# Batches 2 to 6: ScalarE's double pieces over two rows, the gate's product over two rows

## The reference

```python
xz = einsum('bld,ed->bel', hidden, in_proj_w)          # 1024 x channels, 1024 z channels
x  = silu(conv4(x) + conv_b)                           # causal, 4 taps, per channel
dt_lo, Bmat, Cmat = split(einsum('bdl,kd->blk', x, x_proj_w))   # 32, 16, 16
delta = softplus(dt_lo @ dt_proj_w.T + dt_proj_b)
h = h * exp(delta * A) + delta * B_t * x_t             # for each token, 16 states a channel
y = sum_over_states(h * C_t) + x * D
out = (y * silu(z)) @ out_proj_w.T
x1 = layernorm(hidden + out)
logits = x1 @ gate_w.T                                 # 8 experts
top2, idx = top_k(logits, 2); w = softmax(top2)
y_all = einsum('td,eod->teo', x1, expert_w) + expert_b
result = layernorm(x1 + sum(y_all[idx] * w))
```

## Time and profile before

| | |
|---|---|
| runs | 2264.38, 2264.75, 2259.15 us |
| profiled execution | 2260.66 us, span 2258.9 us |
| mean granted TensorE clock | 0.947 |
| busy share of the span | TensorE 90%, VectorE 88%, GpSimd 82%, ScalarE 73% |
| the five periods of batches 2 to 6 | from 561.2 to 1863.0 us of the span |

### The profile page before, as it was taken

How to read it: one execution, slowest core, us unless ns; L and a number is a source line. 1 busy time by engine, 2 the same in 40 slices (tenths; PEclk the granted TensorE clock), 3 DMA queues, 4 the chain that set the end, 5 groups by cost and what they waited for, 6 DMA issues and landing times. The chain is left out here.

```text
span 2258.9 us, 30428 instructions
## 1 busy us (share of the span) xinstructions
PE 2036.0 (90%) x8624; PEld 1200.9 (53%) x8624; DVE 1982.8 (88%) x2191; ACT 1658.4 (73%) x3074; POOL 1854.5 (82%) x1505
## 2 busy tenths in 40 slices
PE   8897779898999989999899998999899998879898
PEld 3444455455564555545555555645556455655453
DVE  5899989989999999899999999899998998989912
ACT  5767858767598866979588875988678886667534
POOL 2988999788998889889898889989898997696503
PEclk9897879989899999999999999999999999789999
DMA  5432142367754786557863678557855576495775
GB/s 164 160 108 70 40 148 77 95 212 229 246 126 124 231 289 180 137 171 233 280 172 106 209 249 264 118 153 248 293 150 136 176 245 236 146 272 189 246 270 117
DMA packets 222085, 412.79 MB, mean 183 GB/s; under 512 B 29880, under 2 KB 36152, under 8 KB 221920
## 3 DMA queue, kind: packets, MB, share of 16 engines
q1 hardware_dynamic: 180448, 322.36, 42.6%
q0 software_dynamic: 20496, 57.16, 12.4%
q10 hardware_dynamic: 20976, 31.33, 4.3%
HBM read 299.37 MB, written 85.72 MB: 170 GB/s over the span
## 5 line engine op out<-in xcount | busy, mean ns | idle before, releaser
L1784 ACT ACTIVATE dA<-delta,negA 128x512 f32<-128x512 f32 (+1 forms) x1146 | 714.4, 637 | 317.4 <-DVE hst L1976 250.1
L1925 POOL TENSOR_TENSOR hst<-u,Bbc 128x512 f32<-128x512 f32 x666 | 880.7, 1427 | 57.4 <-PE hTp L1334 36.3
L1976 DVE TENSOR_TENSOR_SCAN hst<-dA,hst 128x512 f32<-128x512 f32 x672 | 790.3, 1207 | 44.0 <-ACT dA L1784 36.8
L1334 PEld LDWEIGHTS hTp<-ident,hst 128*128 128x128 f32 x4096 | 496.2, 149 | 318.4 <-issue 172.2
L1334 PE MATMUL hTp<-ident,hst 128*128 128x128 f32 x4096 | 557.9, 288 | 96.5 <-DVE hst L1976 24.4
L1965 DVE SCALAR_TENSOR_TENSOR y<-hTp,Ct,y 128x1024 f32<-128x1024 f32 x463 | 585.1, 1264 | 54.5 <-PE hTp L1334 51.6
L1925 POOL TENSOR_TENSOR first_dbu<-u,Bbc 128x512 f32<-128x512 f32 x222 | 295.1, 1411 | 16.5 <-DVE hits L2057 11.6
L1976 DVE TENSOR_TENSOR_SCAN hst<-dA,first_dbu 128x512 f32<-128x512 f32 x224 | 263.2, 1207 | 17.7 <-issue 9.1
L1318 PE MATMUL bank<-wslot,hidT 128*128 128x512 f32 x512 | 250.3, 621 | 8.1 <-ACT zs L1666 6.2
L1318 PE MATMUL bank<-wslot,tokT 128*128 128x512 f32 x496 | 233.3, 598 | 4.0 <-ACT tokT L1686 3.9
L1318 PE MATMUL bank<-delta,tokT 128*128 128x512 f32 x480 | 224.4, 600 | 0.0
(11 more groups left out here) (187 smaller groups left out, 2886.7 us busy)
## 6 DMA issues: line engine op xcount, KB each, us to landing
wslot<-in_w_expT SPq DMA_DIRECT2D x90, 1024.0 KB
Bbc<-b_scratch SPq DMA_DIRECT2D x113, 256.0 KB
wslot<-in_w_inT SPq DMA_DIRECT2D x26, 1024.0 KB
y<-scaled POOLq DMA_DIRECT2D x49, 512.0 KB
zs<-sorted_tokens ACTq DMA_DIRECT2D x91, 256.0 KB, 6.1
sorted_results<-ysb SPq DMA_DIRECT2D x90, 256.0 KB
res<-in_w_expT SPq DMA_DIRECT2D x18, 1024.0 KB, 5.7
gate_scratch<-zs SPq DMA_DIRECT2D x64, 256.0 KB, 2.8
```

Of the source, the lines that this page charges most:

```text
L1334: mm = nc.tensor.transpose(hTp[q % 2][:, tok(j)], hst[n % 2][:, j, start:start + P], ident[:, :])
L1784: nc.scalar.activation(decay_of(step, halved), delta[w.odd][:, j, cols], ACT.Exp, scale=negA[:, j, n:n + 1]).then_inc(exp_done, 1)
L1925: nc.gpsimd.tensor_tensor(dbu_row(n, j), u[w.odd][:, j, :], Bbc[n % 2][:, :], ALU.mult).then_inc(dbu_done, 1)
L1976: nc.vector.tensor_tensor_scan(hst[n % 2][:, j, :], dA[j % 2][:, :], dbu_row(n, j), 0.0, ALU.mult, ALU.add).then_inc(scan_done, 1)
```

## The change

Three things are changed, all in the table of batches 2 to 6. ScalarE's double pieces are taken apart (`one_by_one`): the first half stays in its row, the second goes to the next row, behind that row's decay; a piece that stood in a row with a scaling moves one row on; later pieces never overtake earlier ones, so they are pushed along. The gate's product is cut in two: token tiles 0 and 1 stay in row 62, 2 and 3 go to row 64 (`gate_in_two_rows`), and the count is issued as two shares of one row, which leaves its instructions as they were. VectorE's gate moves from row 63 to 65 (`moved_on`), and GpSimd's hold, which follows from it, by two rows.

```diff
+SCALED_ROWS = [2 * (q + NH + 1) for q in BY_DMA]
+def one_by_one(pieces, steps):
+    rows, last = [], 0
+    for row, x, _ in pieces:
+        row += row in SCALED_ROWS
+        for k, name in enumerate(SINGLE.get(x[0], (x[0],))):
+            last = min(max(row + k * (last <= row), last), steps - 1)
+            rows.append((last, (name,) + x[1:], 0))
+    return rows
+def gate_in_two_rows(pieces):
+    rows, later = [], []
+    for row, x, share in pieces:
+        if later and row > later[0][0] - 2:
+            rows, later = rows + later, []
+        if x == ("gate",):
+            rows += [(row, x, 0), (row, x, 1)]
+            later = [(row + 2, x, 2), (row + 2, x, 3)]
+        elif x == ("count",):
+            rows += [(row, x, 0), (row, x, 1)]
+        else:
+            rows.append((row, x, share))
+    return rows
+def moved_on(pieces, piece, by):
+    rows, last = [], 0
+    for row, x, share in pieces:
+        last = max(last, row + by * (x == piece))
+        rows.append((last, x, share))
+    return rows
...
-        self.shares = FINE_SHARES if self.fine else SHARES
+        self.single = self.fine or steps == STEPS
+        self.shares = FINE_SHARES if self.single else SHARES
         order, users, turns = plan(pieces, steps, pace, steps > STEPS, self.fine)
+        if self.single and not self.fine:
+            order["pe"] = gate_in_two_rows(order["pe"])
+            order["dve"] = moved_on(order["dve"], ("gate",), 2)
...
+        if self.single and not self.fine:
+            order["act"] = one_by_one(order["act"], steps)
...
                 elif name == "gate":
...
-                    for t in range(NT) if not w.seg.fine else (share,):
+                    for t in range(NT) if not w.seg.single else (share,):
...
-                    if not w.seg.fine:
+                    if not w.seg.single:
                         piece(w, ("sig3", j))
...
```

More of the change, by code:

```diff
@@ L1471, in piece @@
                             mm = nc.tensor.matmul(ps[:, NT * NE:(NT + 1) * NE], ones[:, :], hits[:, t, :], start=(t == 0), stop=(t == NT - 1))
-                    if share == 1 or not w.seg.fine:
+                    if share == 1 or not w.seg.single:
                         for i in range(NT):
```

## The result

The changed kernel takes 2352.19 us, the median of four runs (2337.69 to 2360.73), against 2264.57 us before (2259.15 to 2268.25, four runs): ratio 1.038, 95% interval [1.032, 1.045]. It is slower, as forecast, but 88 us slower and not 60, and the time lies above the range of 2284 to 2345.

A forecast was written before the change was run, and what follows sets the result against it. No engine was the bound everywhere: VectorE set the pace, with waits for short chains through ScalarE or TensorE. Terms of 4.6, 2.2, 3.0, 0.5, 1.7 and 0 made 12.0 us a period, 60 in five: 2324, range 2284 to 2345.

The forecast's parts named there:

- The rule: ScalarE works in order; each row begins with its decay, which waits for the scan two rows earlier, as do pushed pieces.
- The x stage: Rows 77 to 80: x 5 and x 6 evictions come behind decays 79 and 80, delaying VectorE's taps; 4.6 us a period.
- Sig 7 to row 88: Rows 82 to 88: sig 7 behind decay 82 makes GpSimd's product 2.5 us later, delaying row 88; 2.2 us a period.
- The dt stage: Rows 94 to 100: later evictions delay row 98's sum by 0.8 and TensorE at row 100 by 2.2; 3.0 us a period.
- Neither is won back: The delays at rows 98 and 100 stay, as TensorE is packed, 22.7 of 23.0 us up to row 110.
- Row 15: yT 1's eviction moves behind decay 15, so TensorE's turning starts 0.61 later; 0.5 us a period.
- The z stage: z 0's and z 2's copies come behind decays 40 and 48: 1.0; x 0 and x 2, rows 71 to 74: 0.7.
- The gate: VectorE's waits for product and count vanish (-2.7 us a period) or double (+2.7); z 6 wants z 5's bank sooner; taken as 0.
- The clock: TensorE's waits before xproj and moe 2 exceed 3.5 us each; 3.4 us more at the lower clock would cost 1.7 us.
- Rival C: The clock drops after both longer TensorE waits, before xproj and moe 2: 17 us more, 2341; chance 0.08.
- Rival B: Only the x stage counts, the rest absorbed by waits VectorE has anyway: 23 us, 2287; chance 0.13.
- Rival D: Faster: earlier decays return 24 us, half the gate's waits 7, x evictions cost no more than today: 2233; chance 0.06.

The follow-up runs named there:

- x_only: The kernel before with only sig2/sig3 taken apart and row 78's pieces pushed on: ratio 1.020.
- x_back: The changed kernel with row 78's pieces left in row 78 and sig2 and sig3 in one row again: ratio 1.021.
- xsT_late: The kernel before with the evictions of xsT 2 and 3, and dt2 2 behind them, one row later, behind decay 100: ratio 1.008.
- xsT_warm: As xsT_late, with two more 128x512 products of no use on TensorE in its wait before moe 2: ratio 1.006.
- rest: The changed kernel with sig2/sig3, dt/dt1 and dt2/dt3 in one row again and nothing pushed on from rows 78, 94 and 110: ratio 1.010.
- rest_copy: As rest, but with the copy of z 5 back in row 63 beside its first half: ratio 1.004.
- dt_back: The changed kernel with dt and dt1, dt2 and dt3 in one row again and nothing pushed on from rows 94 and 110: ratio 1.030.
- pieces_only: Of the change only ScalarE's pieces taken apart, with the gate as in the kernel before: ratio 1.039.
- later_three: The kernel before with three whole pieces (ln2 0, ln1 2, dt2 1) one row later: ratio 0.997.

## Why the prediction was wrong

The forecast of slower, the rule about the decays and the largest term were right; the size was a third too small. The step that failed is the one on the clock: it put at nothing the lower clock behind TensorE's longer waits.

- **The rule** (each row begins with a decay, so what is pushed on waits for a scan) held in each place shown.
- **The x stage**, forecast 4.6, measured 4.5 (x_only 4.5, undone by x_back).
- **Sig 7 to row 88**, forecast 2.2, measured 3.5, and 3.1 in x_only. The delay was right: GpSimd's product for sig 7 ends 2.6 us later after row 80's scan, forecast 2.5. Row 88's decay waits behind xproj, and xproj took 1.1 us longer on average, at the lower clock; in batch 4 the wait before it had grown from 1.28 to 3.59. That this is the clock's doing is read from the traces; no run kept the clock up here. Batch 4 also was not like the others here, as the prediction took it to be: before the change the clock fell behind the wait of 1.3 us in batches 2 and 4 and stayed whole behind it in 5 and 6.
- **The dt stage**, forecast 3.0, measured 5.9. Its parts: row 98, forecast 0.8, measured 0.8; TensorE's resumption, forecast 2.2, measured 2.3; then 1.6 for the clock at row 100. That the clock falls by the wait and costs about this much is shown by xsT_late and xsT_warm (0.9 to 1.7), and batch 2 of x_back, where it stayed up behind the same wait, is 1.4 to 1.8 shorter than the other four. Then 0.7, net, for GpSimd's wait for dt 4 at row 110, which I never looked for, and 0.4 in small steps from row 100 on. "Neither is won back" was right, but I had read TensorE's packing from row 100 to 110 as the only limit there. Only the trace shows the part at row 110; no run took it away by itself.
- **Row 15**, forecast 0.5, measured 1.3 for rows 0 to 16, of which 0.6 stand between the scans of rows 14 and 16. In rest, rest_copy, x_back, dt_back and pieces_only, all with yT 1 behind decay 15, that step grew by 0.5 to 0.7 too, and by -0.1 to 0.0 in those without. So the term was right; the rest lies ahead of row 14, in waits that differ from period to period, and has no cause shown.
- **The z stage**, forecast 1.0 up to row 60, measured 0.5: z 0's and z 2's copies do delay TensorE, and the decays of rows 46 and 53, which come earlier, take it back by row 53 (1.0 at row 50, 0.0 at row 53, counted from row 38).
- **The gate**, forecast 0, with x 0 and x 2 at 0.7; measured 1.9 together. By the estimate under rest the gate costs 0.8 and the pieces 1.7 in these rows, and the clock, which was low in them for 20.5 us of five periods instead of 27.3, gave 0.7 back in this execution. The prediction named one cause, z 6 wanting z 5's bank, and priced it at nothing; moved back, the copy of z 5 takes 0.4 of the 2.0 that rest has by the same estimate.
- **The clock** is the step that failed. I forecast that TensorE's waits before xproj and moe 2 would be "over 3.5 us each", had before me in the earlier trace rows a wait of 2.44 with the clock at 0.51 behind it, and still took the higher clock for the likely case, because a wait of 1.24 kept it. The kernel before had more to see: behind the wait of 1.28 before xproj the clock fell in two of the four periods that have this wait. Measured: behind moe 2's wait 1.6 us a period, and behind xproj's about 1.1, together some 13 of the 28 us that were missing; shown by experiment is the part at row 100. Rival C, with both waits followed by the lower clock and 17 us for it, got 0.08; its mechanism was the case, and its 2341 was 11 us too low. The rest of the miss is rows 100 to 127 (1.2 a period), the gate's rows (1.2), rows 0 to 14 (0.7) and small parts, less the 0.5 that the z stage cost too little.
- TensorE's 29.1 us of added busy time look like the 27.8 us that were missing, but that is luck. 5.3 of them lie in rows 76 to 80, whose step was 4.5 in every period, with the clock low for 3.4 to 3.6 us in three and never in two; and row 110's part is not the clock's.
- Rival B (absorption) was wrong: the steps come and go whole. Rival D was wrong too: the waits of rows 15, 46 and 53 did go, 12 us in five periods, but rows 47, 63 and 88 now wait 16 us more, and the x evictions cost what the forecast said. What it was right in is shown by later_three.

On the clock the Trainium skill was weighed in the prediction (TensorE: Matmul & The Clock Gate, "HAM oscillation"). By its rule, waits bring the lower clock back in the midst of a kernel. The traces agree: behind the wait of 3.54 us the clock was at or near 0.5 in all five periods of the changed kernel, though in x_back in four of five only. The rule deserved more than a rival's chance.

Not settled: the times of the changed kernel spread over 23 us (2337.69 to 2360.73), those of the kernel before over 9. The periods' rows 60 to 76 differ most (-1.1 to 5.8 us of growth in the changed kernel's trace, -1.0 to 7.2 in dt_back's), and follow the time that the clock stays low after the gate: 3.4, 3.4, 0, 13.7 and 0 us in the changed kernel's five periods. What decides that time was not found. Nor is it shown why the parts measured alone, 1.8% + 2.0% + 1.0%, add up to 4.8% and not to 3.8%; in rest's trace 12 us of its 30 stand in these rows.

## What to carry to other kernels

When an engine works in order and each stretch of its work begins with an instruction that waits, moving a piece behind that instruction costs the whole wait wherever another engine needs the piece at once, and it can only pay for pieces that nobody waits for: list who waits for each moved half before counting what it frees. When a forecast makes a wait of TensorE longer, put the lower clock behind it into the sum, and not among the rivals, if the trace has one such wait with a low clock behind it. And follow each moved piece to all its readers, GpSimd's too, also where another engine looks like the limit.

## What was not expected of the hardware

Work of no use made a kernel faster: two more products of 1.98 us in a wait of TensorE kept the clock at 1.00, and the next stretch of work took 0.9 to 1.7 us less. It stayed slower than the kernel before, which has no such wait. And the fall of the clock behind a wait is not certain: behind five equal waits of 3.54 us in one execution it was 1.00 once and 0.50 to 0.60 four times. Nor did it take a long one: behind the wait of 1.28 us before xproj in the kernel before it fell twice in four.
